# Flamingo block with a routed feed-forward on one core: the shared expert cut into an up stage and a down stage, the result table read by tile pair

## What is computed

```python
x = x + tanh(g_xattn) * cross_attention(layernorm(x), ctx)     # x: 32 x 64 x 512, so 2048 tokens
x = x + tanh(g_ffn) * ffn(layernorm(x))
# ffn, on 2048 tokens of width 512:
scores = softmax(xt @ router_w + router_b) + router_bias       # 16 experts, 4 groups, best 2 groups, best 2 experts
y = sum over the 2 chosen experts e of score_e * ((silu(xt@w1[e]+b1[e]) * (xt@w2[e]+b2[e])) @ w3[e] + b3[e])   # inner width 128
z = (silu(xt@sw1+sb1) * (xt@sw2+sb2)) @ sw3 + sb3              # the shared expert, inner width 256
return y + z
```

## Time and profile before

| | us |
|---|---|
| median of 3 runs | 1564.21 (1564.15 to 1565.78) |
| the profiled execution's own time | 1563.39 |
| its span, first to last instruction | 1561.6 |
| TensorE busy in the span | 1480.0 |
| DVE busy | 984.3 |
| ACT busy | 777.0 |
| POOL busy | 186.8 |

### The profile page before, as it was taken

The page is one execution under the profiler, slowest core; times in us unless marked ns, Lnnn a source line. Parts: engine busy times, 40 slices in busy tenths (PEclk is TensorE's granted clock), DMA queues, the critical chain, the costliest instruction groups (busy, mean ns, idle before and its releaser), DMA issues.

```text
span 1561.6 us, 26321 instructions
## 1 busy us (share of the span) xinstructions
PE 1480.0 (95%) x9136; PEld 1311.9 (84%) x9136; DVE 984.3 (63%) x1646; ACT 777.0 (50%) x2022; POOL 186.8 (12%) x198
## 2 busy tenths in 40 slices
PE   7999989999999999999999999999999988888896
PEld 5888878999999999899999989999998677777874
DVE  5322237666677666576766667766667588666648
ACT  3112226555566555455655545655555434667750
POOL 0000000000000000000000000000005312767740
PEclk9999999999999999999999999999999989999998
DMA  7576542121222112222221123211102104777437
GB/s 239 158 223 162 149 148 102 48 68 40 88 92 92 42 48 66 76 68 75 75 68 41 47 83 114 69 48 48 67 16 81 49 21 146 245 231 239 135 107 276
DMA packets 97447, 163.67 MB, mean 105 GB/s; under 512 B 12435, under 2 KB 47287, under 8 KB 93258
## 3 DMA queue, kind: packets, MB, share of 16 engines
q1 hardware_dynamic: 87370, 145.62, 28.8%
q0 software_dynamic: 9984, 16.82, 3.4%
HBM read 128.29 MB, written 49.81 MB: 114 GB/s over the span
## 4 chain that ended last, share of the span: by engine, by line
PE 66%; issue 6%; DVE 6%; ACT 3%; DMA 2%; SPq 2%; another core or an unknown queue 1%; ACTq 0%; POOL 0%; POOLq 0%; DVEq 0%
PE ps_q L84 8%; PE ps_q L86 8%; PE ps_q L85 8%; PE ps_y L85 8%; PE ps_y L84 8%; PE ps_y L86 8%; PE ps_s L1008 5%; PE ps_p L1048 4%; PE ps_o L84 2%; PE ps_s L1010 2%; PE ps_o L86 2%; PE ps_o L85 2%; DMA w_raw<-in_L_ffn_ew 1%; DVE y L1951 1%; DVE y L1205 1%
## 5 line engine op out<-in xcount | busy, mean ns | idle before, releaser
L84 PE MATMUL ps_q<-xt,wq_hi 128*128 128x256 f32 x1024 | 302.5, 295 | 4.4 <-PEq L118 4.4
L86 PE MATMUL ps_q<-xt,wq_hi 128*128 128x256 f32 x1024 | 291.7, 285 | 0.0
L85 PE MATMUL ps_q<-xt,wq_lo 128*128 128x256 f32 x1024 | 291.7, 285 | 0.0
L842 ACT ACTIVATE s_sb<-s_sb,nmax 128x128 f32<-128x128 f32 x512 | 199.9, 392 | 130.5 <-DVE nmax L924 130.5
L922 DVE TENSOR_TENSOR s_sb<-ps_s,s_cross 128x512 f32<-128x512 f32 x128 | 88.5, 691 | 231.4 <-ACT s_cross L831 231.4
L831 ACT ACTIVATE s_cross<-ps_s 128x512 f32<-128x512 f32 x128 | 76.5, 597 | 271.1 <-PE ps_s L1010 271.1
L84 PE MATMUL ps_y<-wo_hi,o_hi 128*128 128x512 f32 x512 | 202.4, 395 | 0.9 <-DVE y L902 0.9
L86 PE MATMUL ps_y<-wo_lo,o_hi 128*128 128x512 f32 x512 | 202.6, 396 | 0.0
L85 PE MATMUL ps_y<-wo_hi,o_lo 128*128 128x512 f32 x512 | 202.6, 396 | 0.0
L84 PEld LDWEIGHTS ps_q<-xt,wq_hi 128*128 128x128 f32 x1024 | 196.9, 192 | 5.0 <-issue 4.8
L85 PEld LDWEIGHTS ps_q<-xt,wq_lo 128*128 128x128 f32 x1024 | 197.2, 193 | 0.0
(11 more groups left out here) (264 smaller groups left out, 3254.9 us busy)
## 6 DMA issues: line engine op xcount, KB each, us to landing
xt<-x_scratch SPq DMA_DIRECT2D x32, 1024.0 KB, 4.9
w_raw<-in_L_ffn_ew SPq DMA_DIRECT2D x93, 256.0 KB
v_full<-v_out SPq DMA_DIRECT2D x64, 128.0 KB, 2.6
k_full<-k_out SPq DMA_DIRECT2D x16, 512.0 KB, 2.8
w_raw<-in_L_xattn_Wq SPq DMA_DIRECT2D x16, 512.0 KB, 5.3
kt_raw<-k_full SPq DMA_DIRECT2D x32, 256.0 KB, 2.7
vt_raw<-v_full SPq DMA_DIRECT2D x32, 256.0 KB, 2.7
w_raw<-in_L_xattn_Wo SPq DMA_DIRECT2D x16, 512.0 KB, 4.2
```

The source lines that it names most:

```text
L84: pe.matmul(out, w_hi, x_hi, start=first, stop=False)
L85: pe.matmul(out, w_lo, x_hi, start=False, stop=False)
L86: return pe.matmul(out, w_hi, x_lo, start=False, stop=last)
L842: last = act.activation(s_sb[:, i], s_sb[:, i], ACT.Exp, bias=nmax[:, i:i + 1], accum_out=sums[:, i:i + 1])
```

## The change

`SharedHalf` is replaced by one `SharedExpert` with eight jobs j (octet j // 2, half j % 2).

- All eight jobs' up products now stand in front of the slots, on TensorE as `pe_up(j, k)`. Their `h` parts are kept in SBUF, in the space of `x_hi` and `x_lo` that the up products have already read.
- All down products stand behind the slots. One tile is one sum of seven products (two halves of three passes, and the `b3` product), in eight PSUM banks, with one `dve_add` per tile. Before it was two sums and two adds per tile.
- The split of the second half's weights moves ahead of the routing, and so do their loads on SP (to the store of tile 10).
- TensorE turns tiles 12 to 15 before it turns the logits back, and no up product stands among the last logits any more. `logits_t` lies in `rows_in`, so POOL clears `rows_in[0]` only after the logits are turned.
- The split of `b3` moves from the middle of the routing to behind it.
- ACT waits for the low part of all eight jobs before its slot loop.
- In the tail the table is loaded as eight tile pairs, each 2 DMAs of 512 KB with a semaphore of its own. DVE adds the down products of tiles 0 to 7 first, then for each pair its two table rows, and in between the down products of tiles 8 to 15. Stores wait for the pair (`y_done`).

The core of the diff:

```diff
@@ copy_logits
-        if o == 3:
+        if o == 0:
             act.wait_ge(self.signals["weighted"], 128)
@@ class SharedExpert (new)
+    JOBS = 2 * OCTETS
+    DEEP = 4
+    def split_high(self, act, half, raw):
+        act.wait_ge(self.raw_in[half], 48)
+        act.activation(self.up[half][0][:], raw[:, 0:2], ACT.Copy)
+        act.activation(self.down[half][0][:], raw[:, 2], ACT.Copy).then_inc(self.w_hi_made, 1)
+    def act_up(self, act, j):
+        r, half = j % self.DEEP, j % 2
+        act.wait_ge(self.up_done, j + 1)
+        if j >= self.DEEP:
+            act.wait_ge(self.h_lo_made, j - self.DEEP + 1)
+        act.activation(self.silu[r][:], self.pair(j)[0][:], ACT.Silu, bias=self.bias[:, 0, half:half + 1])
+        act.activation(self.h_sb[r][:], self.pair(j)[1][:], ACT.Identity,
+                       bias=self.bias[:, 1, half:half + 1]).then_inc(self.gate_copied, 1)
+    def act_high(self, act, j):
+        act.wait_ge(self.h_made, j + 1)
+        act.wait_ge(self.up_done, j // 2 * 2 + 2)
+        act.activation(self.h[j // 2][j % 2][0][:], self.h_sb[j % self.DEEP][:], ACT.Copy).then_inc(self.h_hi_made, 1)
+    def dve_product(self, dve, j):
+        dve.wait_ge(self.gate_copied, j + 1)
+        dve.tensor_tensor(self.h_sb[r][:], self.silu[r][:], self.h_sb[r][:], ALU.mult).then_inc(self.h_made, 1)
+    def dve_low(self, dve, j):
+        dve.wait_ge(self.h_hi_made, j + 1)
+        dve.tensor_tensor(h_lo[:], self.h_sb[j % self.DEEP][:], f32(h_hi[:]), ALU.subtract).then_inc(self.h_lo_made, 1)
+    def dve_add(self, dve, n, gain):
+        dve.wait_ge(self.down_done, n + 1)
+        dve.scalar_tensor_tensor(out=self.y[:, n, :], in0=self.ps_down[n % 8][:], scalar=gain[:],
+                                 in1=self.y[:, n, :], op0=ALU.mult, op1=ALU.add).then_inc(self.y_added, 1)
+    def pe_up(self, pe, j, k, lo=0, hi=C):
+        if k == 0 and lo == 0:
+            if j < 2:
+                pe.wait_ge(self.w_lo_made, half + 1)
+            elif j == self.JOBS - 1:
+                pe.wait_ge(self.gates_copied, OCTETS)
+            else:
+                pe.wait_ge(self.gate_copied, j - 1)
...
+    def pe_down(self, pe, n):
+        bank, tokens = self.ps_down[n % 8], slice(n % 4 * P, n % 4 * P + P)
+        if n >= 8:
+            pe.wait_ge(self.y_added, n - 7)
+        for half in range(2):
+            h_hi, h_lo = self.h[n // 4][half]
+            three_pass(pe, bank[:], h_hi[:, tokens], h_lo[:, tokens], self.down[half][0][:], self.down[half][1][:],
+                       half == 0, False)
+        pe.matmul(bank[:], self.stacked[:, P * n:P * n + P], self.b3[:], start=False, stop=True
+                  ).then_inc(self.down_done, 1)
@@ sync
+                if n == 10:
+                    sp.wait_ge(signals["scored"], 128)
+                    shared.load(sp, a, 1, sw_raw[1])
...
-            sp.wait_ge(logits_turned, OCTETS)
-            shared[1].load(sp, a, sw_raw[1])
...
-            for o in range(OCTETS):
+            for q in range(TILES // 2):
                 for i in range(2):
-                    for g in range(2):
-                        sp.dma_start(y2[o][i][g], choices_v[o, i, g]).then_inc(y2_in[o], 16)
-            for n in range(0, TILES, 2):
-                sp.wait_ge(shared[1].y_added, n + 2)
-                sp.dma_start(out_v[n // 2], y[:, n:n + 2, :]).then_inc(stored, 16)
+                    sp.dma_start(y2[q][i], choices_v[q, i]).then_inc(y2_in[q], 16)
+            for q in range(TILES // 2):
+                sp.wait_ge(y_done, q + 1)
+                sp.dma_start(out_v[q], y[:, 2 * q:2 * q + 2, :]).then_inc(stored, 16)
@@ gpsimd
+            pool.wait_ge(logits_turned, OCTETS)
             pool.memset(rows_in[0][:], 0.0).then_inc(consts_made, 1)
@@ scalar
             scalar_two(act)
+            act.wait_ge(signals["halves"], 128)
+            for r in range(2):
+                act.wait_ge(xn_stored[r], 32)
+            shared.split_high(act, 1, sw_raw[1])
             front.copy_logits(act, 1)
...
+            shared.act_up(act, 0)
+            shared.act_up(act, 1)
+            shared.act_up(act, 2)
+            gates_high(0)
+            gates_high(1)
+            shared.act_up(act, 3)
+            gates_high(2)
+            gates_high(3)
+            act.wait_ge(b3_in, 32)
+            act.activation(b3[0:32], b3_raw, ACT.Copy)
+            act.activation(b3[32:64], b3_raw, ACT.Copy).then_inc(small_hi_made, 1)
+            shared.act_high(act, 0)
+            shared.act_high(act, 1)
+            shared.act_up(act, 4)
+            shared.act_high(act, 2)
+            shared.act_up(act, 5)
+            shared.act_high(act, 3)
...
             act.wait_ge(slots_made, 3)
+            shared.act_high(act, 4)
             w_up_high(0, 0)
             w_down_high(0, 0)
+            shared.act_up(act, 6)
+            shared.act_high(act, 5)
             xs_high(0, 0)
+            shared.act_up(act, 7)
+            shared.act_high(act, 6)
+            shared.act_high(act, 7)
+            act.wait_ge(shared.h_lo_made, shared.JOBS)
             over_slots(act, slot)
             evacuate(LAST, LAST % 2)
-            for o in range(OCTETS):
-                shared[1].act_job(act, o)
@@ vector
             for n in range(12, TILES):
                 front.x_low(dve, n)
+            shared.split_low(dve, 1, sw_raw[1])
...
-            dve.wait_ge(small_hi_made, 5)
-            dve.tensor_tensor(b3[64:96], b3_raw, f32(b3[0:32]), ALU.subtract).then_inc(small_lo_made, 1)
...
-            for o in range(2):
-                shared[0].dve_h_product(dve, o)
-            shared[0].dve_h_low(dve, 0)
-            shared[1].dve_split(dve, sw_raw[1])
+            shared.dve_product(dve, 0)
+            shared.dve_product(dve, 1)
+            shared.dve_low(dve, 0)
+            shared.dve_low(dve, 1)
...
-            shared[0].dve_h_low(dve, 1)
-            shared[0].dve_add(dve, 0, gain)
+            shared.dve_product(dve, 2)
+            shared.dve_product(dve, 3)
...
+            shared.dve_low(dve, 2)
+            shared.dve_low(dve, 3)
+            dve.wait_ge(small_hi_made, 5)
+            dve.tensor_tensor(b3[64:96], b3_raw, f32(b3[0:32]), ALU.subtract).then_inc(small_lo_made, 1)
+            shared.dve_product(dve, 4)
+            shared.dve_product(dve, 5)
+            shared.dve_low(dve, 4)
...
             w_up_low(0, 0)
             w_down_low(0, 0)
-            shared[0].dve_add(dve, 2, gain)
+            shared.dve_low(dve, 5)
             xs_low(0, 0)
-            shared[0].dve_add(dve, 3, gain)
+            shared.dve_product(dve, 6)
+            shared.dve_product(dve, 7)
+            shared.dve_low(dve, 6)
+            shared.dve_low(dve, 7)
             over_slots(dve, slot)
...
+            for n in range(8):
+                shared.dve_add(dve, n, gain)
+            for q in range(TILES // 2):
+                dve.wait_ge(y2_in[q], 32)
                 for i in range(2):
...
+                    dve.tensor_tensor(y[:, 2 * q:2 * q + 2], y[:, 2 * q:2 * q + 2], y2[q][i],
+                                      ALU.add).then_inc(y_done if i else y2_added, 1)
+                if q < 4:
+                    shared.dve_add(dve, 8 + 2 * q, gain)
+                    shared.dve_add(dve, 9 + 2 * q, gain)
@@ tensor
+            for n in range(12, TILES):
+                front.turn(pe, n)
             for o in range(2):
                 front.turn_logits(pe, o)
-            for n in range(12, TILES):
-                front.turn(pe, n)
...
-            shared[0].pe_up_part(pe, 0, 0, 0, 2)
             front.logits(pe, 3, small_lo_made)
-            front.turn_logits(pe, 2)
-            shared[0].pe_up_part(pe, 0, 0, 2, 3)
-            front.turn_logits(pe, 3)
-            shared[0].pe_up_part(pe, 0, 0, 3, C)
-            shared[0].pe_up_part(pe, 0, 1, 0, C)
+            for o in range(2, OCTETS):
+                front.turn_logits(pe, o)
+            for part in range(2):
+                shared.pe_up(pe, 0, part)
...
             # then up(1), up(2, 0) | ranks | up(2, 1), gates 0, 1, up(3), gates 2, 3
             # | hot q=0, up(4, 0), q=1, up(4, 1), q=2, up(5, 0), q=3, up(5, 1)
             # | slot biases, up(6) | turn slot 0, up(7), slots
...
             down(LAST, LAST % 2)
...
+            for n in range(TILES):
+                if n in (3, 6):
+                    pe.wait_ge(y_out_made, 2 * SLOTS - 2 if n == 3 else 2 * SLOTS)
+                shared.pe_down(pe, n)
```

More of the change, by code:

```diff
@@ L1279, in stage_three @@
         }
-        work = [[b.sb(f"s_{name}{i}", [P, 512], dt) for i in range(2)]
+        biases = [b.sb(f"biases{i}", [P, 2]) for i in range(2)]
+        with ExitStack() as up_front:
+            e = Buffers(nc, up_front)
+            s_silu = [e.sb(f"s_silu{i}", [P, 512]) for i in range(SharedExpert.DEEP)]
+            s_h_sb = [e.sb(f"s_h_sb{i}", [P, 512]) for i in range(SharedExpert.DEEP)]
+        work = [[b.sb(f"{name}{i}", [P, 512], dt) for i in range(2)]
```

(7 more changed lines are left out.)

289 lines of the change are left out of this document (98 added, 191 removed).

## The result

| | before | changed |
|---|---|---|
| median (on the same chip) | 1564.99 us (1564.15 to 1569.67) | 1544.51 us (1542.62 to 1548.22) |
| the profiled execution's own time | 1563.39 | 1544.32 |
| its span | 1561.6 | 1542.6 |

The ratio is 0.9868, with a 95% interval of 0.9845 to 0.9892: the change is worth 1.3%. The prediction said 1544.7.

A forecast was written before the change was run, and what follows sets the result against it. DVE was taken to pace most of the old head and the tail, all engines sharing the slots. Profiled 1563.4 - 9.4 (head) - 10.1 (tail) = 1543.9, plus 0.8 for the median: 1544.7 us; range 1539.5 to 1555.

The forecast's parts named there:

- Rival A: Whole kernel: both head and tail pay, 1544.7 us, from 1541.5 to 1549; chance 0.68.
- Step 1: Head, last logits: nine up products (2.1 us) and small turning products (0.4) move, so routing starts 2.5 earlier, at 1245.4.
- Step 2: Head, ranks: DVE waits for TensorE; ranks take 3.3 us and end at 1262.7, so 1.1 of the 2.5 are left.
- Step 3: Head, one-hot rounds: DVE stays the pace, its 3.13 us wait goes, and the last matrix is done at 1284.3.
- Step 4: Head, slot numbers: they start at 1286.9 and experts are known at 1289.9, 5.3 us earlier.
- Step 5: Head, up to slot 1: TensorE paces, slot 1's up products start 10.4 us earlier, at 1309.7; ACT's wait costs 2.1.
- Step 6: Head, TensorE's clock: two half-clock stretches vanish, one appears before slot 1; gain taken as 1.0 us, between 0 and 2.
- Tail: After the slots: DVE's adds end at 1548.1, last store takes 3.3 us, end 1551.4, gain 10.1.
- The transfers' bound: Tail, DMA: 12.6 MB at 390 from 1518 takes 32.3 us, to 1550.3, just beneath DVE's end with store, 1551.4.
- B: Slots swallow the head's gain, waiting for slot 2's weights or rows; 1554.1 us, half of it 1549.4; chance 0.12.
- C: Tail: pair loads do not land in order of issue, so the tail gives nothing; 1554.8 us; chance 0.07.
- D: Head: TensorE at half clock makes the kernel slower, 1583 us with all 192 up products slow; chance 0.05.

The follow-up runs named there:

- e6: Changed kernel with TensorE's old order: two octets of logits turned ahead of tiles 12 to 15, nine up products among the last logits; 1546.16 us, ratio 0.9891.
- e4: Changed kernel with job 5's half between the third and fourth one-hot rounds moved behind the fourth on TensorE; 1546.09 us, ratio 0.988.
- e5: Changed kernel with slot 1's rows and up weights prepared on ACT and DVE ahead of the last shared high and low parts; 1546.49 us, ratio 0.988.
- e7: Changed kernel with six shared adds, not eight, ahead of the first table pair and two behind each of the first five pairs; 1548.19 us, ratio 0.9869.
- e1: Changed kernel with DVE waiting for both pairs of an octet before its first loaded add; 1535.92 us, ratio 0.9868.
- b1: Kernel before, with only its first octet loaded and added by tile pair; 1565.17 us, ratio 0.9999.
- e9: Changed kernel with jobs 4 and 5 whole behind the four one-hot rounds, no up products between rounds; 1555.78 us, ratio 0.9909.
- e2: Changed kernel with two shared adds ahead of the loaded adds and the other 14 two by two behind the pairs; 1540.58 us, ratio 0.9908.
- a1: Changed kernel unaltered, run again on the chip of e7, e8 and e9; 1546.70 us, ratio 0.9864 to the kernel before.
- e8: Changed kernel with the edits of e4, e5 and e7 at once; 1545.95 us, ratio 0.9858.
- a0: Changed kernel unaltered, run again on the chip of e1, e2 and e3; 1535.78 us, ratio 0.9879 to the kernel before.
- e3: Changed kernel with each shared add in the tail done a second time into a buffer nobody reads; 1542.27 us, ratio 0.9916.
- group 1: The tail runs a0, e1, e2 and e3, on one chip, where the kernel before took 1555.89 us.

## Why the prediction was right, step by step

**The total.** 1544.7 forecast; 1544.51 measured beside the kernel before, on 1564.99; by ratio 1564.21 x 0.9868 = 1543.6. Rival A. The head was to give 9.4 and gave 8.2 at slot 0's result (8.3 at slot 1), the tail 10.1 and gave 9.8, and 2.1 came from the spread of the slots less 1.1 of stage two. So the two parts together came out 1.5 us under the forecast. That the profiled execution agrees with it more closely (1543.9 against 1544.32) is luck: the spread gave 1.0 back.

**Step 1, routing 2.5 earlier:** 2.3 (and 2.3 by e6, which undoes it).

**Step 2, ranks end at 1262.7, 1.1 earlier; DVE then waits for TensorE:** 0.9 earlier and DVE waits 2.21. Right by two errors that cancel. The 3.3 us for the ranks were a row at half clock; at full clock they take 1.85 (1262.07). And 1.6 us were lost to the clock dip in the jobs ahead, which I had not in this place. Without the dip the ranks are done 2.5 earlier.

**Step 3, "DVE stays the pace":** this step failed. DVE's own length was right (ranks to the last one-hot matrix 21.9, forecast 5.1 + 16.5 = 21.6), and so was the vanished wait of 3.13. But I set 12 products, 2.8 us, against DVE's round and left out the round's own 16 products, 1.8 us. With them TensorE needs 4.6 a round, for the rounds from 1274.45 to 1290.16, and DVE, through with its four other operations, waits 1.73 for the last. The four slowed operations cost 0.97 to 1.10 each (1.77 against 0.67 at L1861), 4.1 together. The Trainium skill, SBUF — State Buffer, section SBUF: two separate sides, says that whichever of the two starts first keeps the shared ports for its whole instruction and the other blocks. The trace agrees, more closely than I had read it for the prediction: POOL's four subtractions end at 1271.46, 1273.15, 1277.98 and 1279.65, and DVE's operations 0.53 us after the first three and 1.08 after the last, which is a longer one (1.22 alone). So the delay is what is left of POOL's instruction when DVE's begins, 1.1 to 1.2 us here less 0.1, and not its full length.

**Step 4, experts 5.3 earlier:** 3.1 measured. 1.7 of the missing 2.2 are that wait. It did not matter: e4 brings the experts 1.8 forward and slot 1 stays where it is, since the same error had let TensorE idle "some 2 us for the experts" in my count, and the measured wait is 0.3. The products that I had forgotten fill most of the idle time that I had counted.

**Step 5, slot 1 10.4 earlier before the clock:** 9.9 without a dip. The price of ACT's wait, 2.1, was right at slot 1 (e5: 1.7, or 1.9 with its slightly later ranks taken off), but slot 1 was the wrong place to end the count. By the traces the loop follows slot 0's `y_out` through POOL's queue.

**Step 6, 1.0 for the clock:** 1.6, in the first jobs of the routing and not before slot 1. The first two stretches that fell away were longer than the 4 us that I had read from the earlier trace rows, 6.8 each.

**Tail.** DVE through with tiles 0 to 7 at 15.5 us after the last slot's down products: 15.4. DVE's end 39.4: 39.9. Last store 3.3 after it: 3.2. The transfers' bound was to lie "just beneath", at 1550.3 or 41.6; in e7 DVE ends 1.05 sooner and the tail still takes 43.1, so the bound lies beside DVE's, 1.5 above where I had it. The mis-sized term is the 2 us of latency: 2 us and 2.1 MB at the full rate make 7.4, not the 8.8 that I had read, and the last load of the changed kernel landed 24.9 us after the first issue, 3.4 more than the 21.5 of the rate. "A pair is in 2.7 sooner" was too little (5.5 after its issue against 9.2 for two in e1), but only 1.4 of it could be used (e1), and on the kernel before it is worth nothing (b1).

**Rivals.** B, that the slots swallow the head's gain, is refuted by e9 for a shift of the whole head and fits e5, where a shift of slot 1 alone is gone by slot 4. C did not happen: pairs landed in order, 5.5 and 10.2 us after the first issue in e2, and in the changed kernel none was waited for. Single loads did change places: by the semaphores of the trace the fifth (of the third pair) landed 9.93 us after the first issue in e2 and the fourth (of the second pair) 10.19, and 10.09 and 10.38 in e9. That agrees with the Trainium skill, DMA: Bandwidth & Descriptors, section Queues, rings and completion order, by which completion isn't first in, first out. D: the clock in the head is 1.00 but for one dip, so it didn't happen.

## What to carry to other kernels

When two engines feed each other in rounds, add up on each side everything that stands in its list within a round, the exchanged product itself included; the larger sum is the pace. Before a head's gain is booked, follow it to the instruction that releases the steady loop (here a scatter ahead of a gather in one in-order queue) rather than to the first work of the loop. Check a wait's slot number against the list: here slot 4 waited for slot 5's rows. Where an edit brings one of two nearly equal bounds down, the other one takes over within a microsecond: e7 freed DVE and met the transfers.

## What the hardware showed that I had not expected

TensorE's clock fell in the head of the changed kernel without an idle stretch of TensorE before it. TensorE in short stretches (busy, granted clock, DMA):

```profile
1242.70:1246.70 4.00, 4.00 (x26) 1.00 0.00 0
1246.70:1250.70 4.00, 4.00 (x13) 0.64 0.00 0
1250.70:1254.70 4.00, 4.00 (x18) 0.93 0.00 0
```

Just ahead stand 32 small turning products (32x16) in two groups of 1.95 us, one on either side of the last logits. In six of eleven executions with the new order of turns (changed, a1, e2, e5, e7, e8) the clock then fell to 1.2 GHz for some 3.5 us and the ranks came 1.6 us later; a0, e3, e4 and e9, with the same list up to there, kept 2.4 GHz, and e1 fell earlier and lost 4.7 us. So it isn't decided by the list alone. In the three executions with the old order (before, b1, e6), where the small products stand in groups of 16, 8 and 8 with other products between them, it did not fall there. The Trainium skill, TensorE: Matmul & The Clock Gate, section Part 1: The HAM clock gate (the "warmup" mystery), ties the clock to how busy TensorE has been of late. No run here took the small products away, so whether they are behind the fall isn't shown.

The kernel's slots ran some 6% faster on the chip of group 1 than on the others (177.8 to 179.6 us from slot 1 to the last down products against 186.5 to 194.2), with the same instructions. The experiments don't say why.
